# A selective scan on one Trainium2 core: delta and y summed by TensorE, du replicated through DRAM

## The reference

```python
x0 = x.reshape(B, D, L)
x1 = x.transpose(0, 1, 3, 2).reshape(B, D, L)
xs = jnp.stack([x0, x1, x0[..., ::-1], x1[..., ::-1]], axis=1)
x_dbl = jnp.einsum('bkdl,kcd->bkcl', xs, x_proj_weight)
dts, Bs, Cs = jnp.split(x_dbl, [R, R + N], axis=2)
dts = jnp.einsum('bkrl,kdr->bkdl', dts, dt_projs_weight)
A = -jnp.exp(A_logs.astype(jnp.float32)).reshape(K, D, N)
delta = jax.nn.softplus(dts + dt_projs_bias[None, :, :, None])
def step(h, inp):
    u_t, d_t, B_t, C_t = inp
    h = jnp.exp(d_t[..., None] * A) * h + (d_t * u_t)[..., None] * B_t[:, :, None, :]
    y = jnp.einsum('bkdn,bkn->bkd', h, C_t)
    return (h, y)
...
ys = ys.transpose(1, 2, 3, 0) + Ds.reshape(K, D)[None, :, :, None] * xs
ym = ys[:, 0:2] + ys[:, 2:4][..., ::-1]
y = ym[:, 0] + ym[:, 1].reshape(B, D, W, H).transpose(0, 1, 3, 2).reshape(B, D, L)
```

## Time and profile before

| | us |
|---|---|
| median of 3 runs | 6593.33 (6592.84 to 6594.92) |
| profiled execution, its own time | 6584.0 |
| its span | 6581.8 |
| TensorE busy | 5493.3 (83%) |
| VectorE busy | 5359.4 (81%) |
| GpSimd busy | 4218.5 (64%) |
| ScalarE busy | 2742.5 (42%) |

### The profile page before, as it was taken

How to read it: one execution, slowest core, us unless ns; L and a number is a source line. 1 busy time by engine, 2 the same in 40 slices (tenths; PEclk the granted TensorE clock), 3 DMA queues, 4 the chain that set the end, 5 groups by cost and what they waited for, 6 DMA issues and landing times. The chain is left out here.

```text
span 6581.8 us, 69145 instructions
## 1 busy us (share of the span) xinstructions
PE 5493.3 (83%) x15890; PEld 2653.9 (40%) x15890; DVE 5359.4 (81%) x5305; ACT 2742.5 (42%) x4050; POOL 4218.5 (64%) x2650
## 2 busy tenths in 40 slices
PE   7999798976999888806788888888888888888887
PEld 2222364642666555503333333333333333333332
DVE  4768434342199999998799998999989999899997
ACT  5767434332000000002455554555545555455555
POOL 0000323223098777896788887888878888788883
PEclk9989899988999888958899998999989999899999
DMA  1000000038555666503011111111111111011111
GB/s 41 0 0 0 7 1 0 1 109 226 119 124 124 129 131 132 111 0 85 23 34 29 34 31 28 34 29 34 32 27 34 29 34 34 25 34 32 32 34 49
DMA packets 105200, 330.99 MB, mean 50 GB/s; under 512 B 19980, under 2 KB 36808, under 8 KB 91112
## 3 DMA queue, kind: packets, MB, share of 16 engines
q1 hardware_dynamic: 104936, 328.05, 20.9%
HBM read 170.81 MB, written 56.51 MB: 35 GB/s over the span
## 5 line engine op out<-in xcount | busy, mean ns | idle before, releaser
L1747 POOL TENSOR_TENSOR l_hc<-l_h,l_c_rep 128x512 f32<-128x512 f32 x1536 | 1977.7, 1301 | 292.0 <-DVE l_h L1810 265.2
L1810 DVE TENSOR_TENSOR_SCAN l_h<-l_p_da,l_h,l_bu 128x512 f32<-128x512 f32 x1344 | 1701.0, 1266 | 0.0
L1588 PE MATMUL l_p_y<-l_hc,l_y_pick 128*96 128x512 f32 x3072 | 1639.5, 616 | 17.6 <-POOL l_hc L1747 10.8
L1674 ACT ACTIVATE l_p_da<-l_p_da,l_a_neg 128x512 f32<-128x512 f32 x1536 | 1010.2, 659 | 1531.0 <-PE l_p_da L1581 1529.5
L1578 PE MATMUL l_p_du<-l_stacked,l_pick 96*128 96x512 f32 x1536 | 1200.5, 782 | 181.4 <-DVE l_bu L1800 152.9
L1146 POOL TENSOR_TENSOR l2b_prod<-l2b_v,l2b_attn 128x3136 f32<-128x3136 f32 x114 | 990.5, 8704 | 392.5 <-ACT l2b_attn L1138 369.7
L1800 DVE TENSOR_TENSOR l_bu<-l_p_du,l_b_rep 128x512 f32<-128x512 f32 x1536 | 1015.5, 661 | 18.1 <-PE l_p_da L1581 17.3
L1581 PE MATMUL l_p_da<-l_stacked,l_pick 96*128 96x512 f32 x1536 | 732.5, 477 | 253.6 <-DVE l_h L1810 247.7
L1581 PEld LDWEIGHTS l_p_da<-l_stacked,l_pick 96*128 96x128 f32 x1536 | 304.2, 198 | 930.2 <-DVE l_h L1810 841.0
L1180 DVE TENSOR_REDUCE l2b_osum<-l2b_prod 128x64 f32<-128x3136 f32 x192 | 645.9, 3414 | 2.7
L1578 PEld LDWEIGHTS l_p_du<-l_stacked,l_pick 96*128 96x128 f32 x1536 | 301.6, 196 | 737.6 <-DVE l_bu L1800 499.2
(11 more groups left out here) (241 smaller groups left out, 8380.5 us busy)
## 6 DMA issues: line engine op xcount, KB each, us to landing
l_stacked<-l_parts SPq DMA_DIRECT2D x512, 192.0 KB, 3.2
l2b_img_high<-qkv_scratch SPq DMA_DIRECT2D x192, 306.2 KB, 5.5
l2b_img_low<-qkv_scratch SPq DMA_DIRECT2D x192, 306.2 KB, 9.2
qkv_scratch<-l2a_strip SPq DMA_DIRECT2D x32, 840.0 KB, 5.1
l2b_v<-qkv_scratch SPq DMA_DIRECT2D x48, 560.0 KB, 17.0
qkv_scratch<-l2a_v_strip SPq DMA_DIRECT2D x32, 210.0 KB, 4.0
x_front<-x SPq DMA_DIRECT2D x4, 1536.0 KB, 18.6
x_scratch<-x_front SPq DMA_DIRECT2D x4, 1536.0 KB, 14.6
```

Of the source, the lines that this page charges most:

```text
L1588: pe.matmul(p_y[par][:], y_pick[:, g, :], hc[:, g % HCS, :], start=(g == 0), stop=(g == G - 1)).then_inc(s_ymm, 1)
L1674: act.activation(p_da[g % DAS][:], p_da[g % DAS][:], ACT.Exp, scale=a_neg[:, k * G + g:k * G + g + 1]).then_inc(s_da, 1)
L1747: pool.tensor_tensor(hc[:, g % HCS, :], h[:, g, :], c_rep[:, par, :], ALU.mult).then_inc(s_hc, 1)
L1810: dve.tensor_tensor_scan(h[:, g, way], p_da[g % DAS][:, way], bu[:, g % DAS, way], state, ALU.mult, ALU.add).then_inc(s_h, 1)
```

## The change

All of it is in the scan stage, but for a block that clears semaphores ahead of the back half and the buffer du_d in DRAM.

- delta is summed in PSUM by TensorE: identity times relu, identity times (e - kept), identity times log, the bias -log 1 being added when ScalarE reads it (`delta_sum`, `delta_and_high`, `rest`). VectorE's `delta` is gone.
- du is not replicated by TensorE. GpSimd writes it whole, SP stores it in DRAM and reads each group's 8 rows back 16 times over, into a ring of 8 tiles (`store_du`, `replicate_du`). Only delta is restacked.
- B's projection stays in PSUM (p_b), C's is still copied.
- The y products come three at a time (`y_triple`); groups are taken in the order GRP. The running y or D * u is added by one more product (`y_whole`), and ScalarE takes the result (`take_y`). VectorE's `add_y` and `image_end` are gone.
- The loops run on over the images; x is transposed piece by piece (`turn_x`).

Of the diff, the added lines of the new parts with their context follow (the removed ones are those of the functions printed above). SP:

```diff
+            def store_du(m, par):
+                sp_.wait_ge(s_du, m + 1 + DU0)
+                sp_.nop(nofuse=True)
+                sp_.wait_ge(s_bu, G * (m - 1) + BU0)
+                sp_.nop(nofuse=True)
+                sp_.dma_start(du_d[par], du[:]).then_inc(s_dus, 16)
+            def replicate_du(n, par, i):
+                if i == 0:
+                    sp_.wait_ge(s_dus, 16 * (n + 1) + DUS0)
+                    sp_.nop(nofuse=True)
+                sp_.wait_ge(s_bu, G * n + (i + 1 - RING) + BU0)
+                sp_.nop(nofuse=True)
+                src = du_d[par, GRP[i] * DL:(GRP[i] + 1) * DL]
+                src = bass.AP(src.tensor, src.offset, [[0, S], [N, DL], [1, N]])
+                sp_.dma_start(du_rep[:, ring_at(par, i)], src).then_inc(s_dur[ring_at(par, i)], 16)
...
+            def step(n, par, more):
+                for i in range(RING, G):
+                    replicate_du(n, par, i)
+                    if more and i == RING:
+                        store_du(n + 1, 1 - par)
+                    if more and i == RING + 1:
+                        sp_.wait_ge(s_rep, G * n)
+                        sp_.nop(nofuse=True)
+                        restack(n + 1, 1 - par)
+                if more:
+                    for i in range(RING):
```

TensorE:

```diff
+            def b_mm(m, par, b, k, c):
+                pe.wait_ge(s_bu, G * (m - 1) + BU0)
                 pe.nop(nofuse=True)
+                pe.matmul(p_b[par][:], w_rep[:, k, 0, :], u_of(b, k, c), start=True, stop=True).then_inc(s_b, 1)
+            def delta_sum(m, copied):
+                if copied is not None:
+                    pe.wait_ge(s_ccp, copied + CCP0)
                     pe.nop(nofuse=True)
+                pe.wait_ge(s_relu, m + 1)
+                pe.nop(nofuse=True)
+                pe.matmul(p_bc[0:C, :], ident[:], relu_x[:], start=True, stop=False)
+                pe.wait_ge(s_rest, m + 1)
+                pe.nop(nofuse=True)
+                pe.matmul(p_bc[0:C, :], ident_r[:], rest_e[:], start=False, stop=False)
+                pe.wait_ge(s_log, m + 1)
+                pe.nop(nofuse=True)
+                pe.matmul(p_bc[0:C, :], ident[:], log_e[:], start=False, stop=True).then_inc(s_d, 1)
...
+            def replicate(n, i, par):
+                pe.wait_ge(s_h, G * n + i + 1 - DAS + H0)
+                pe.matmul(p_da[i % DAS][:], pick[:, GRP[i] % (Q // DL), :], stacked[:, par, GRP[i] * DL // Q, :],
                           start=True, stop=True).then_inc(s_rep, 1)
...
+            def y_triple(n, t, par):
+                pe.wait_ge(s_hc, G * n + YT * t + YT + HC0)
+                if t == 0:
                     pe.wait_ge(s_y, n - 1 + Y0)
...
+            def y_whole(n, b, k, c, par):
+                at = chunk_of(k, c)
+                pe.wait_ge(s_y, n + Y0)
+                pe.nop(nofuse=True)
+                if k == 0:
+                    mm = pe.matmul(p_y[par][:], d_diag[:], u_of(b, k, c), start=False, stop=True)
+                elif k == 2:
+                    mm = pe.matmul(p_y[par][:], ident[:], y_sum[:, bass.ds(at * N, N)], start=False, stop=True)
+                else:
+                    mm = pe.matmul(p_y[par][:], ident[:],
+                                   y_sum[:].rearrange("c (y x) -> c x y", x=W)[:, bass.ds(at * COLS, COLS), :],
+                                   start=False, stop=True)
+                mm.then_inc(s_ysum, 1)
...
+                for i in range(G):
+                    replicate(n, i, par)
+                    if before and i == 0:
+                        y_triple(n - 1, 2, 1 - par)
+                    if n2 and i == 1:
+                        dt_mm(n + 2, *n2, n + 1)
+                    if n1 and i == 2:
+                        b_mm(n + 1, 1 - par, *n1)
+                    if before and i == 3:
+                        y_triple(n - 1, 3, 1 - par)
+                    if before and i == 4:
+                        y_whole(n - 1, *before, 1 - par)
+                    if n1 and i == 5:
+                        c_mm(n + 1, *n1, n2)
+                    if i == 6:
+                        y_triple(n, 0, par)
+                    if n2 and i == 8:
+                        delta_sum(n + 2, n + 2)
+                    if i == 9:
+                        y_triple(n, 1, par)
```

ScalarE:

```diff
+            def delta_and_high(m, par):
+                act.wait_ge(s_d, m + 1)
+                act.nop(nofuse=True)
+                act.wait_ge(s_du, m + DU0)
+                act.nop(nofuse=True)
+                act.wait_ge(s_lo, m + LO0)
+                act.nop(nofuse=True)
+                act.activation(dd[:], p_bc[0:C, :], ACT.Identity, bias=ln_one[:])
+                restacked(m - 1, 1 - par)
+                act.activation(parts[:, 0, :], p_bc[0:C, :], ACT.Identity, bias=ln_one[:]).then_inc(s_hi, 1)
...
+            def take_y(n, b, k, c, par):
+                at = chunk_of(k, c)
+                act.wait_ge(s_ysum, n + 1)
+                act.nop(nofuse=True)
+                if k in (0, 2):
+                    act.activation(y_sum[:, bass.ds(at * N, N)], p_y[par][:], ACT.Copy).then_inc(s_y, 1)
+                else:
+                    whole = y_sum[:] if k == 1 else X[:, bass.ds(b * HW, HW)]
+                    act.activation(whole.rearrange("c (y x) -> c x y", x=W)[:, bass.ds(at * COLS, COLS), :],
+                                   p_y[par][:].rearrange("c (x y) -> c x y", y=H), ACT.Copy).then_inc(s_y, 1)
...
+            def step(b, n, k, c, par, n1, n2, before):
+                for i in range(G):
+                    decay(n, k, i)
+                    if n2 and i == 2:
+                        abs_relu(n + 2, n2[1])
+                    if n2 and i == 3:
+                        exp_x(n + 2)
+                    if n2 and i == 4:
                         one_plus(n + 2)
                         kept(n + 2)
+                    if n2 and i == 5:
                         log_1e(n + 2)
+                    if n1 and i == 6:
+                        c_copy(n + 1, 1 - par)
+                    if before and i == 7:
+                        take_y(n - 1, *before, 1 - par)
+                    if n2 and i == 10:
+                        delta_and_high(n + 2, par)
+                    if k == 0 and i == 8:
+                        if not isinstance(c, int):
+                            turn_x(b, c + 2)
+                        elif c < 2:
+                            act.wait_ge(s_du, n + 1 + DU0)
+                            act.nop(nofuse=True)
+                            turn_x(b, 2 * c)
+                    if k == 0 and isinstance(c, int) and c < 2 and i == 9:
+                        turn_x(b, 2 * c + 1)
```

GpSimd and VectorE:

```diff
+            def rest(m):
                 pool.wait_ge(s_kept, m + 1)
                 pool.nop(nofuse=True)
+                pool.wait_ge(s_d, m)
                 pool.nop(nofuse=True)
+                pool.tensor_tensor(rest_e[:], e_x[:], kept_e[:], ALU.subtract).then_inc(s_rest, 1)
+            def delta_u(m, b, k, c):
+                pool.wait_ge(s_hi, m + 1 + HI0)
                 pool.nop(nofuse=True)
...
+            def low(m, par):
+                pool.wait_ge(s_hi, m + 1 + HI0)
+                pool.nop(nofuse=True)
+                if not (isinstance(m, int) and m == 0):
+                    pool.wait_ge(s_stack[1 - par], stacked_by(m - 1, 1 - par))
                     pool.nop(nofuse=True)
...
+            def times_c(n, i, par):
+                if i == 0:
+                    pool.wait_ge(s_ccp, n + 1 + CCP0)
+                pool.wait_ge(s_h, G * n + i + 1 + H0)
+                pool.wait_ge(s_ymm, TRIPLES * n + (i - HCS) // YT + 1 + YMM0)
+                pool.tensor_tensor(hc[:, (G * par + i) % HCS, :], h[:, i, :], c_rep[:, par, :], ALU.mult).then_inc(s_hc, 1)
+            def step(b, n, k, c, par, n1, n2, before):
+                if k == 0 and isinstance(c, int) and c == CHUNKS - 1:
+                    pool.wait_ge(s_xt, CHUNKS * b + CHUNKS)
+                    pool.nop(nofuse=True)
+                for i in range(G):
+                    if n1 and i == 0:
+                        low(n + 1, 1 - par)
+                    if n1 and i == 2:
+                        delta_u(n + 1, *n1)
+                    times_c(n, i, par)
+                    if n2 and i == 6:
+                        rest(n + 2)
...
+            def times_b(b, n, i, par):
+                if i == 0:
+                    dve.wait_ge(s_b, n + 1)
+                dve.wait_ge(s_dur[ring_at(par, i)], 16 * (G // 4 * (n - par) // (RING // 4) + (G * par + i) // RING) + 16)
+                dve.wait_ge(s_h, G * n + i + 1 - BUS + H0)
+                dve.tensor_tensor(bu[:, i % BUS, :], du_rep[:, ring_at(par, i)], p_b[par][:], ALU.mult).then_inc(s_bu, 1)
...
+            def step(b, n, k, c, par, n1, n2, before):
+                for i in range(G):
+                    if i < G - 1:
+                        times_b(b, n, i + 1, par)
                     elif n1:
```

(58 more changed lines are left out.)

362 lines of the change are left out of this document (132 added, 230 removed).

## The result

The changed kernel takes 6628.34 us (median of 8 runs, 6614.53 to 6644.03), the kernel before, run beside it, 6594.28: a ratio of 1.005, 95% interval 1.0039 to 1.0061. It is 0.5% slower, which this measurement tells from no change. Forecast was 6468.

A forecast was written before the change was run, and what follows sets the result against it. VectorE was taken to bound a scan step, with TensorE's new wait and clock bringing it to 24.4 us; 128 steps make 3123, 127 under 3250, ends +2: 6459, plus 9.3 for the median, 6468 us. Range 6300 to 6700.

The forecast's parts named there:

- VectorE's part: Scan loop: delta and y sums leave VectorE, nothing is added, products with B stay at 661 ns.
- the floor that was given: Scan step on VectorE: 12 product-and-scan pairs of 1.773 us, so no step shorter than 21.28 us.
- The new wait: TensorE, before delta's rest product in each step, idles 3.3 us for GpSimd's rest of e, delaying the replications behind it.
- The lateness at full clock: Scans 9, 10 and 11 late by 0.8, 1.0 and 0.1 us; step 23.2 us if TensorE keeps its clock.
- Its clock: TensorE behind the new wait: one half-clock stretch of 3.4 us costs 1.5 us in 8 of 10 steps, 1.2 us; step 24.4.
- The second stretch: Rival: half clock behind TensorE's wait persists beyond one stretch; two cost about 3.0 us, step 26.2, total 6699; chance 0.14.
- the stated break-even of 25.4: Step length, 3250 / 128 us, above which the changed scan stage is slower: 2.2 us lost to the clock.
- not under 3: Sign of a right forecast: VectorE's idle stretches before scans 9 and 10, under 3 us in sum per step.
- Seams and ends: Between images 87 us of seams go; stage end takes 5.5 us instead of 8.5, start adds 5; ends +2.
- DMA: Replicating reads of du in the scan loop cost nothing; a step moves about 3.7 MB, 17 us of 24.4.
- the 0.6 given as a sign: Sign of a right forecast: DMA busy share in the scan loop of 0.6 to 0.75.
- Its rival with VectorE as only bound: Rival: TensorE's wait hurts nothing in the scan loop; step 21.3 us, total 6071; chance 0.05.

The follow-up runs named there:

- both moves: Changed kernel with GpSimd's rest of e behind its product of group 5 instead of 6 and TensorE's delta sum behind replication of group 10 instead of 8: 6066.5 us.
- three products of fill: Changed kernel with relu's product of delta's sum issued three more times just before TensorE waits for the rest of e: 6339.8 us.
- The rest early alone: Changed kernel with GpSimd's rest of e behind its product of group 5 instead of 6: 6158.2 us.
- the later sum: Changed kernel with TensorE's delta sum behind replication of group 10 instead of 8, and ScalarE's reading of it behind exp 11 instead of 10: 6065.4 us.
- the last experiment: Kernel before the change, with VectorE's own delta recurrence one group later (group 10 instead of 9): 6456.7 us.

## Why the prediction was wrong

Point by point, against the profiled execution (6629.6 us; the sum gave 6459):

- **VectorE's part: right.** A pair is still 1.773 us: 4526.52 - 4521.20 = 5.32 for three (starts of VectorE's products with B). The removed work went, and both moves reach 21.28 us a step, the floor that was given.
- **The new wait: right in place and size.** 3.3 us forecast, 3.0 measured, for GpSimd's rest.
- **The lateness at full clock: right.** Scans 9 and 10 late by 1.9 in sum gave 23.2 us; with the clock kept (three products of fill) it is 23.40, and most steps there have scan 9 late by 1.04 and scan 10 by 0.95.
- **Its clock: the step that failed.** "I take 1.5 in 8 of 10 steps, 1.2 us". Measured: 2.29 us a step. One stretch does cost 1.7 (1.68), as worked out, but five of nine steps have a second behind it and lose 3.19: (4 x 1.68 + 5 x 3.19) / 9 = 2.5, near the 2.29. The second stretch stood as a rival for every step, at 26.2 us (chance 0.14), with, against it, "Today every stretch I saw in the loop ends once TensorE is busy". The forecast also puts the stretch around 4485.0 to 4487.5 behind the idling of 1.51 and 0.69 us in the earlier trace rows. That idling leads into another one, from 4508.8; the one it names follows idling of 0.79 and 0.63 us, which end at 4482.37 and 4483.50. Neither was evidence for what follows 3 us. With 25.69 the step passed the stated break-even of 25.4, and the two scans are late by 4.3 us in sum, not under 3.
- **Seams and ends.** The seams did go: the changed kernel's first late scan behind 4032 us waits 2.26 us, as in any step. The start of the scans moved by +7.7 us instead of +5 (3249.0 against 3241.3), and the end kept its length (6627.9 - 6537.5 = 90.4 against 90.6) instead of losing 3: 6 us in all. The start alone says little: in the edits of the changed kernel it lies anywhere from 3237.8 to 3254.4. The step's 1.3 us more than 24.4 make 165, together the 171 between sum and measurement.
- **DMA: right that it costs nothing.** No wait for du_rep in the loop, though a read lands in 4.3 us in the changed kernel (share 0.57, 145 GB/s) and in 4.9 with both moves (0.70, 174 GB/s). The share of 0.7 at 24.4 us a step was too high; 0.57 is also under the 0.6 given as a sign. 146 GB/s was the rate under which the DMAs would decide; 174 were reached without a wait. The Trainium skill ("DMA: Bandwidth & Descriptors", Anatomy of one DMA) would give 2.6 us for one of these by an estimate, from its fit for the GpSimd path. These are issued by SP with several under way and take 4.3, so the estimate doesn't fit them; in this order it did not matter.
- **Not seen by the forecast:** that the stall was only a matter of order. The working had what was needed: rest ready at 2.60, and the replication and the triple queued behind it. Its rival with VectorE as only bound (6071) names a condition, "GpSimd's rest early", and both moves came to 6066. The rest early alone gave 6158; the later sum, which the forecast did not think of, gave 6065 without it.

Why a step gets one spell or two is open; in the nine windows above the two kinds mostly alternate, behind nearly the same wait. In the step from 4522.5 the clock fell to half only within 4526 to 4527, after the rest product had begun (4525.77); in the step before it was at half from 4499 on, just before that product began (4499.26).

## What to carry to other kernels

Before work is moved onto an in-order engine, find when its last input is ready, and put the instruction behind the work that feeds the bound and is ready before it; here this was worth 562 us. Where a wait of that engine lies ahead of the critical chain, price the chain at full clock and at half for its whole length, and take the first as the answer only for a wait that rows of the kernel show to be harmless. The second is a bound: here it would be 4.1 us a step, and 2.3 were lost. A wait on the old kernel's bound may also be mended by its order alone: try that first, as the baseline of the larger change.

## What the runs showed of the hardware

- Useless work can pay: three spare products of 0.87 us each a step raised the granted clock from 0.90 to 1.00 and took 289 us off. By the table, waits of 1.35 us a step left it at 0.99, of 2.17 and 2.71 at 0.94 and 0.93, of 3.03 at 0.90; in the kernel with both moves TensorE waits up to 1.4 us ahead of a replication and keeps 1.00.
- A delta sum on VectorE has no fixed length: 734 to 3790 ns in the last experiment (median 839), 0.77 us in the step shown though GpSimd was working. So the forecast's reading, that the 0.75 us of the seam came from GpSimd standing still, is only one case. The Trainium skill ("SBUF — State Buffer", SBUF: two separate sides) states that whichever of the two engines starts first keeps the other out for a whole instruction; two sums of the kernel before agree with that. Both start 0.1 us behind a GpSimd product (1.27 us). The one at 4479.97 us lasts 1.74 us, and GpSimd's second product comes after it; the one at 4454.46 lasts 2.96, and both products run first, in 2.50 us. Why GpSimd's second product gets in ahead in one step and not in the next is open.
- A DMA that reads eight rows of DRAM sixteen times over (256 KB), with several under way, lands in 4.3 us at 145 GB/s and a share of 0.57 (changed kernel), and in 4.9 us at 174 GB/s and 0.70 (both moves).
